# Attention row sums on Trainium2: a unit's last pair merged by DMA, two row sums a unit, the inverses moved

## The reference

```python
scores = jnp.einsum('bqhs,bkhs->bhqk', q, k) / np.sqrt(HEAD_DIM)
scores = jnp.where(context_mask[:, None, None, :], scores, -jnp.inf)
attn = jax.nn.softmax(scores, axis=-1)
out = jnp.einsum('bhqk,bkhs->bqhs', attn, v).reshape(B, Tx, C)
```

## Time and profile before

| what | us |
|---|---|
| median of 3 runs | 4442.11 (4439.8 to 4442.43) |
| the profiled execution | 4433.29 |
| its span, first to last instruction | 4431.5 |
| PE, DVE, ACT, POOL busy | 4264.6, 3400.1, 2850.1, 2938.9 |

### The profile page before, as it was taken

The page is one execution under the profiler, slowest core; times in us unless marked ns, Lnnn a source line. Parts: engine busy times, 40 slices in busy tenths (PEclk is TensorE's granted clock), DMA queues, the critical chain, the costliest instruction groups (busy, mean ns, idle before and its releaser), DMA issues.

```text
span 4431.5 us, 89201 instructions
## 1 busy us (share of the span) xinstructions
PE 4264.6 (96%) x36496; PEld 1486.4 (34%) x36496; DVE 3400.1 (77%) x3967; ACT 2850.1 (64%) x5184; POOL 2938.9 (66%) x1830
## 2 busy tenths in 40 slices
PE   4999999999999999999999999999999999999998
PEld 2322343223432234322342223422234222342223
DVE  5788667886688865888658886688866888668875
ACT  3387744877448864478655886558755587546884
POOL 2299652996539954499534995359953599426993
PEclk9999999999999999999999999999999999999999
DMA  5256642657326573356733566335664366543654
GB/s 182 71 121 125 158 143 62 125 119 187 115 62 128 115 200 102 71 117 124 191 101 77 115 125 184 106 79 119 124 174 110 78 122 127 167 112 78 126 124 107
DMA packets 193708, 539.67 MB, mean 122 GB/s; under 512 B 28737, under 2 KB 102785, under 8 KB 152082
## 3 DMA queue, kind: packets, MB, share of 16 engines
q0 software_dynamic: 43776, 318.79, 36.0%
q1 hardware_dynamic: 149522, 215.17, 15.6%
HBM read 118.32 MB, written 21.01 MB: 31 GB/s over the span
## 4 chain that ended last, share of the span: by engine, by line
PE 66%; DVE 20%; ACT 4%; DMA 3%; POOL 3%; issue 3%; SPq 0%; DVEq 0%; ACTq 0%; POOLq 0%
PE banks L1114 17%; PE banks L1126 16%; PE banks L1022 16%; PE banks L1082 11%; DVE max_parts L663 11%; PE banks L1157 4%; PE banks L991 2%; ACT region L892 2%; DMA sums<-wkT_wvT_wqT 1%; PE banks L1016 1%; POOL wkT_wvT_wqT L453 1%; DVE amax L611 1%; ACT values L972 1%; DVE x_stats L573 1%; DVE region L801 1%
## 5 line engine op out<-in xcount | busy, mean ns | idle before, releaser
L663 DVE TENSOR_REDUCE max_parts<-banks 128x2 f32<-128x1024 f32 x2048 | 2397.1, 1217 | 409.4 <-PE banks L1082 393.4
L892 ACT ACTIVATE region<-banks 128x512 f32<-128x512 f32 x4096 | 2190.5, 607 | 452.5 <-PE banks L1114 401.6
L453 POOL TENSOR_TENSOR wkT_wvT_wqT<-region 128x1024 f32<-128x1024 f32 x528 | 1313.0, 2632 | 464.6 <-PE banks L1126 273.0
L1114 PE MATMUL banks<-queries_stacked,keys_stacked 98*32 98x512 f16 x16384 | 1264.2, 382 | 12.5 <-ACT values L876 6.2
L1126 PE MATMUL banks<-region,values 128*32 128x512 f32 x8192 | 1076.0, 599 | 17.7 <-ACT region L892 14.2
L1082 PE MATMUL banks<-keys_stacked,queries_stacked 33*128 33x512 f16 x4096 | 724.0, 385 | 31.8 <-DVE max_parts L663 28.3
L1114 PEld LDWEIGHTS banks<-queries_stacked,keys_stacked 98*32 98x32 f16 x16384 | 401.3, 95 | 1000.3 <-ACT region L892 599.4
L1022 PE MATMUL banks<-region,wkT_wvT_wqT 128*128 128x512 f16 x2304 | 556.7, 380 | 13.2 <-DMA wkT_wvT_wqT<-weights_split 10.6
L1082 PEld LDWEIGHTS banks<-keys_stacked,queries_stacked 33*128 33x128 f16 x4096 | 184.2, 93 | 649.1 <-issue 354.1
L453 POOL TENSOR_TENSOR sums<-region 128x1024 f32<-128x1024 f32 x144 | 373.0, 2729 | 9.1 <-ACT region L892 9.1
L433 POOL TENSOR_TENSOR region<-row_sums_inverse,region 128x512 f16<-128x512 f32 x80 | 93.0, 1163 | 429.5 <-ACT region L855 428.9
(11 more groups left out here) (99 smaller groups left out, 3232.4 us busy)
## 6 DMA issues: line engine op xcount, KB each, us to landing
wdT<-wkT_wvT_wqT POOLq DMA_DIRECT2D x96, 1024.0 KB, 12.0
wkT_wvT_wqT<-wkT_wvT_wqT POOLq DMA_DIRECT2D x80, 1024.0 KB, 7.3
sums<-wkT_wvT_wqT POOLq DMA_DIRECT2D x72, 1024.0 KB, 7.4
wkT_wvT_wqT<-sums POOLq DMA_DIRECT2D x40, 1024.0 KB, 7.4
region<-in_x SPq DMA_DIRECT2D x24, 1024.0 KB, 8.6
wkT_wvT_wqT<-weights_split SPq DMA_DIRECT2D x8, 3072.0 KB, 20.6
keys_stacked<-region SPq DMA_DIRECT2D x384, 64.0 KB, 2.0
keys_stacked<-sums SPq DMA_DIRECT2D x384, 64.0 KB, 2.0
```

Of the source, the lines that this page charges most:

```text
L453: e.tensor_tensor(SUMS[dst][:, half], PR[i][:, half], PR[i + 1][:, half], ALU.add).then_inc(s_pr, 1)
L663: e.tensor_reduce(mpart[:, buf, :, a, t, c], MXB[parity], AX.X, ALU.max).then_inc(s_mxd, 1)
L892: e.activation(PR[u % 4][:, j * HALF:j * HALF + HALF], score_bank(m % NU, kt, j)[0], ACT.Exp, scale=SCALE).then_inc(s_ex, 1)
L1114: mm = e.matmul(dst[HD * t:HD * t + HD, :], KA[0:STR, ds(ka + (j * C + (u + 1) * P + HD * t), HD)], QA[0:STR, ds(qa[j], HALF)], start=True ...
```

## The change

- `buffers(n)` names six buffers. The last pair (tiles 14 and 15) goes into `sixth`, which is 5, 0 or 3 in turn, and `first`, `three` and `sixth` change places from unit to unit.
- A new `merge_pair` on GpSimd, at the start of units 1 to 6, merges the unit before's `sixth` into its `first` by an accumulating DMA. It stands right behind `merge_last`, and both now stand ahead of pair 0; `merge_last` stood between the halves of pair 0.
- PE makes two row sums in units 1 to 6: `SUMS[4]` in step 4, and `first` in step 5, when `merge_pair` has landed (`s_ap`).
- GpSimd normalises between the halves of pair 2, and pair 3 waits for `s_ap`.
- VectorE inverts the sums of the unit before last behind the maxima of step 4. In unit 6 the inverse of the unit before stays behind the next unit's maxima.
- The banks of the scores take turns a little differently: the stretch with two banks begins at tile 5 in place of 4.

```diff
-            if tile < 4:
+            if tile < 5:
                 return bank((7, 4, 5)[(4 * tile + j) % 3]), 3
...
-            return [(0, 1, 2, 3, 4), (3, 1, 0, 2, 4), (2, 1, 3, 0, 4)][n % 3]
+            if n == NU - 1:
+                return 3, 1, 0, 2, 4, None
+            first, three, last = [(0, 3, 5), (3, 5, 0), (5, 0, 3)][n % 3]
+            return first, 1, 2, three, 4, last
...
+                        def merge_pair():
+                            into, *_, src = buffers(2 * g + q - 1)
+                            e.wait_ge(s_acc, 3 * n * 16)
+                            e.wait_ge(s_pt, 2 * (b * (NU - 2) + 2 * g + q))
+                            e.dma_start(SUMS[into], SUMS[src], accum_op=ALU.add).then_inc(s_ap, 16)
...
-                        pair(0, first, merge_last if g + q > 0 else None)
+                        if g + q > 0:
+                            merge_last()
+                            merge_pair()
+                        pair(0, first)
                         pair(1, one)
                         merge(0, 1, one)
-                        if 2 <= 2 * g + q < NU - 1:
+                        def normalise():
                             e.wait_ge(s_inv, n - 1)
                             ao = AO[:, ds((2 * g + q - 2) * AO_UNIT, HALF)]
                             e.tensor_tensor(ao, ao, RL[:, :], ALU.mult).then_inc(s_an, 1)
-                        e.wait_ge(s_pv, n * KT + 4 + (3 if g + q == 0 else 4))
-                        pair(2, two)
+
                         if g + q > 0:
                             e.wait_ge(s_ac2, late * 16)
+                        pair(2, two, normalise if 2 * g + q >= 2 else None)
+                        if g + q > 0:
+                            e.wait_ge(s_ap, 16 * (b * (NU - 2) + 2 * g + q))
                         pair(3, three)
...
-                                e.tensor_tensor(SUMS[5][:, half], PR[2][:, half], PR[3][:, half],
+                                e.tensor_tensor(SUMS[sixth][:, half], PR[2][:, half], PR[3][:, half],
...
                             max_row(idx + 8 + 2 * t, 1 - q, QT + t)
+
+                            if n >= 2 and t == 0:
+                                invert_first(m - 2)
+                                invert_rest()
...
-                            if n > 0 and t == 2:
-                                invert_first(m - 1)
-                            if n > 0 and t == 3:
-                                invert_rest()
...
-                                if t == 3 and not end:
-                                    fresh = (s_ex, ex + 4 * J + 2)
-                                if t == 4 and not end:
-                                    sums = [(SUMS[5], (s_pt, 2 * (b * (NU - 2) + n)))]
-                                if t == closing:
+                                if t == (8 if end else 4):
                                     sums = [(SUMS[4], (s_ac2, 16 * (b * (2 * NU - 2) + 2 * n)))]
+                                if not end and t == 4:
+                                    fresh = (s_ex, ex + J + 2)
+                                if not end and t == 5:
+                                    sums = [(SUMS[buffers(n - 1)[0]], (s_ap, 16 * (b * (NU - 2) + n)))]
```

More of the change, by code:

```diff
@@ L182, in score_bank @@
                 slot = 4 * (KT * (n - NU + 2) + tile - 9) + j
-                return bank((4, 5, 0, 1, 2, 3)[slot % 6]), 2 if slot < 2 else 6 if slot >= 6 else None
+                return bank((5, 4, 0, 1, 2, 3)[slot % 6]), 2 if slot < 2 else 6 if slot >= 6 else None
             if n == 0 and tile < 8:
@@ L186, in score_bank @@
                 return bank((7, 4, 5)[slot % 3]), 3 if slot > 3 else None
-            if tile < 4:
+            if tile < 5:
                 return bank((7, 4, 5)[(4 * tile + j) % 3]), 3
             if tile < 8 or n == NU - 2:
-                return bank(4 + j % 2), 3 if tile == 4 and j < 2 else 2
+                return bank(5 - j % 2), 3 if (tile, j) == (5, 0) else 2
             slot = 4 * (tile - 8) + j + ((tile, j) >= (10, 2))
-            return bank((7, 4, 5)[slot % 3]), 2 if tile == 10 and j >= 2 else 3
+            return bank((7, 4, 5)[slot % 3]), 2 if tile == 10 and j >= 2 or (tile, j) == (8, 1) else 3
         def buffers(n):
-            return [(0, 1, 2, 3, 4), (3, 1, 0, 2, 4), (2, 1, 3, 0, 4)][n % 3]
+            if n == NU - 1:
+                return 3, 1, 0, 2, 4, None
+            first, three, last = [(0, 3, 5), (3, 5, 0), (5, 0, 3)][n % 3]
+            return first, 1, 2, three, 4, last
         s_w = sem("weights_loaded")
@@ L239, in build @@
         s_pt = sem("last_tiles_paired")
+        s_ap = sem("last_pairs_merged")
         s_wo = sem("out_projection_weights_loaded")
@@ L351, in _ @@
                         if 2 * g + q == NU - 1:
-                            e.wait_ge(s_pv, (b * NU + NU - 2) * KT + 4 + 5)
+                            e.wait_ge(s_pv, (b * NU + NU - 2) * KT + 4 + 6)
                             e.dma_start(WO[:, :, :], woT.rearrange("(c p) n -> p c n", p=P)).then_inc(s_wo, 16)
@@ L456, in pair @@
                                     halfway()
-                        first, one, two, three, second = buffers(2 * g + q)
+                        first, one, two, three, second, sixth = buffers(2 * g + q)
                         end = g == G - 1 and q == 1
@@ L516, in _ @@
                         if 2 * g + q < NU - 2:
-                            if g + q > 0:
-                                e.wait_ge(s_pv, n * KT + 4 + 5)
-                            elif b > 0:
+                            if g + q == 0 and b > 0:
                                 e.wait_ge(s_op, b * TT)
@@ L698, in last_sums @@
                     def last_sums(m):
-                        first, one, two, three, second = buffers(n)
+                        first, one, two, three, second, sixth = buffers(n)
                         late = b * (2 * NU - 2) + 2 * n
@@ L1201, in quad @@
                                     sums = [(PR[3], None)]
-                                if t == (2 if end else 3):
+                                if end and t == 2:
                                     sums = [(SUMS[buffers(n - 1)[0]], (s_acc, 48 * m))]
-                                if t == 3 and not end:
-                                    fresh = (s_ex, ex + 4 * J + 2)
-                                if t == 4 and not end:
-                                    sums = [(SUMS[5], (s_pt, 2 * (b * (NU - 2) + n)))]
-                                if t == closing:
+                                if t == (8 if end else 4):
                                     sums = [(SUMS[4], (s_ac2, 16 * (b * (2 * NU - 2) + 2 * n)))]
+                                if not end and t == 4:
+                                    fresh = (s_ex, ex + J + 2)
+                                if not end and t == 5:
+                                    sums = [(SUMS[buffers(n - 1)[0]], (s_ap, 16 * (b * (NU - 2) + n)))]
                             step(m, n, ex, ka, qa, v, u, t + 1, rows[u], sums=sums, fresh=fresh, closing=t == closing,
@@ L1217, in unit @@
                     ex, ka, v, rows = at(K3, J - 1, g + 1, q, not last)
-                    first, one, two, three, second = (SUMS[i] for i in buffers(n))
+                    first, one, two, three, second = (SUMS[i] for i in buffers(n)[:5])
                     for u in range(3):
```

## The result

The changed kernel takes **4606.65 us** (median of 4 runs, 4603.19 to 4611.13), against 4440.95 for the kernel before, measured beside it (4 runs, 4438.63 to 4442.43): ratio 1.0374, 95% interval 1.0356 to 1.0392. It is slower by 166 us. The forecast was 4512 in a range that ended at 4555: the sign was right, and the size was 95 us too small.

A forecast was written before the change was run, and what follows sets the result against it. The prediction took a closed loop of POOL and the DMA queue as the bound, 45.7 us per unit: 8.7 us more per batch entry, 70 over eight, on 4433.3 gives 4503, plus 8.8 gives 4512 us; range 4485 to 4555.

The forecast's parts named there:

- PE's bound, 42.6 us: One unit on PE alone: 44.26 us less 0.89 for a row sum and 0.77 for the moved inverse.
- the first two steps at 2.5: PE's first two steps of a unit: about 2.5 us each unless POOL holds them, from 2.91 and 2.86.
- The late merge's landing, 12.9: POOL's unit head: the late merge lands 12.9 us after its issue, second in the queue behind another merge.
- what POOL does until then: POOL has nothing to do from 9.9 us after the late merge's issue until its landing, about 3 us per unit.
- X to the start of pair 1: First part of POOL's loop, X being the issue of a unit's late merge: 18.8 us.
- Does PE add to the loop? ... I add nothing.: PE, stalled in step 5 for the new merge, keeps about 1 us in hand against POOL's pair 5: nothing added.
- tenths: PE's waits for ScalarE in steps 3 and 4: some tenths of a us.
- The inverse in step 4 at nothing: VectorE's inverse behind step 4's maxima: cost on PE taken as nothing, covered by the two row sums.
- What POOL's block costs: The wait for the late merge ahead of pair 0, no longer covered by pair 0's first half; whole change 70 us.
- PE's wait decides: Rival: merges landing 3 us later hold PE in step 5, units 2 us longer, about 4608 us; chance 0.10.
- The skill's rule: GpSimd transfers take about 2 us plus bytes at 436 GB/s: 1 MiB merge 4.4, second some 6 us.

The follow-up runs named there:

- e3_inverse: The kernel before with only the inverse and the normalisation moved as in the change: 4425.8 us, ratio 0.9972 to before.
- e5b_inverse_back: The changed kernel with the inverse back behind the maxima of steps 14 and 15, the normalisation left between the halves of pair 2: 4588.1 us.
- e4_block: The kernel before with its one merge_last moved ahead of pair 0, nothing else: 4518.6 us, ratio 1.0183 to before.
- e1_cover: The changed kernel with both merges put back between the halves of pair 0: 4491.8 us, ratio 1.0121 to before.
- e12_late_sum: e1_cover with PE's row sum of the first buffer moved from step 5 to step 7, with banks, copy and waits to match: 4452.2 us.
- e7b_fill_scores: The changed kernel with two real scores ahead of PE's stalls made seven times over in units 1 to 6: 4563.0 us.
- e2_fill: The changed kernel with twelve zero-weight matmuls per unit 1 to 6, ahead of PE's waits in steps 3 and 4: 4622.1 us.

## Why the prediction was wrong, step by step

- **PE's bound, 42.6 us, and the first two steps at 2.5.** The steps came out at 2.46 and 2.58, and the full-clock unit above has PE busy for 42.77. Right.
- **The late merge's landing, 12.9, and what POOL does until then.** Right: median 12.9, mean 12.69 from the issue, and about 3 us of idle time put to it. The step from the landing to pair 0 was mis-sized: POOL issued L481 0.62 us behind the landing (0.3 in the earlier trace rows), and X to the start of pair 1 was 19.2 in place of 18.8: about 21 us of the 103.
- **"Does PE add to the loop? ... I add nothing."** This is the step that failed. I followed PE only from the sixth merge's landing, into step 5, and asked whether it was in time for pair 5. The path that decided starts earlier: pair 0 frees the exponentials' buffer, ScalarE makes tile 4, PE does step 3, and on to tile 11. The chain of the changed kernel's profile goes that way:

```profile
2120.90 0.86 PE banks L1139 x8
...
2129.81 12.87 DMA wdT<-wkT_wvT_wqT
...
2145.31 4.71 POOL woT L457 x2
2150.07 0.47 issue
2150.53 0.60 ACT region L905
2151.18 0.52 PE banks L1127 x4
2151.70 1.71 PE banks L1139 x8
...
2171.51 0.24 PE banks L1127 x4
2171.77 0.61 ACT region L905
2172.38 2.46 POOL wkT_wvT_wqT L457
```

  It goes through PE and ScalarE from 2150.53 to 2172.38 and back to POOL's pair 5, and a step's value matmuls take 1.71 us at its start, where they took 0.86 a little earlier. At full clock "nothing" would have been right: in the 4 loops with no low clock this part takes 22.0 us (21.7 in the sum), and POOL's rows have no idle time in it but for its own pair. But PE stands some 2.5 us in step 3 of each unit (131.3 us of waits for ScalarE in the whole kernel), the granted clock drops to 1.2 GHz in 42 of 48 loops, and the part is then 1.0 to 2.8 us longer. I had called the waits in steps 3 and 4 "tenths" and asked nothing of what standing does to the clock. It makes up 80 of the 103 us that the loops are over their forecast; the clock's part of the miss is 44 to 66 us.
- **The inverse in step 4 at nothing.** Right for PE and wrong for POOL, whose normalisation waits for it where the clock is low, about 0.5 us a loop, a term that the chain had at nothing: e3_inverse shows the gain by itself, e5b_inverse_back a loss of 18.5 us beside the blocked pair 0.
- **What POOL's block costs.** Right in the main: e4_block, the block alone, costs 82 us, where the forecast had 70 for the whole change.
- **The rival "PE's wait decides"** had the time (4608) by luck, and half the place: PE did decide, but in step 3 for ScalarE, and not in step 5 for a merge 3 us late. The sixth merge landed at X + 26.1 where I had 26.4. Its price shows only with the block away: 74 us of waits in e1_cover, of which e12_late_sum takes 40 us out of the time.
- **The skill's rule** that I had weighed against the change's slowness (Trainium skill, DMA: Bandwidth & Descriptors, Anatomy of one DMA) was not borne out: the merges of 1 MiB landed after 6.9 us at the least, where the estimate by it was 4.4, and right behind another merge after 11.4 to 13.5, where it was some 6.

Three things stay open. The price of the clock lies between 44 and about 66 us. What else makes the loops longer than forecast at full clock, 0.5 us each in the changed kernel's own and 1.1 in e7b_fill_scores (46.83, of the loops that normalise), is located and not explained: POOL's start behind the landing, 0.3 us more of waiting for its own pair 1 (2574.95 to 2580.54 is 5.59 us in a loop with no low clock, where the sum had 5.27), and the two issues ahead of the next X, of which the first is followed by the second after 0.92 us in that loop, where the sum had 0.59. And in e12_late_sum PE's wait in step 3 was found and not tried.

## What to carry to other kernels

A wait put ahead of work is priced by following every engine that the work behind it releases, from that work on and not from the added instruction, and by asking what TensorE does meanwhile: where it stands for some us in each turn, the next rows may have to be reckoned at half the clock as well. Here 42 of 48 loops fell to it with PE standing for ScalarE 131 us in all, and 9 of 48 in e4_block with the same block, a row sum still in step 3 and 37.5 us of such waits. And a change of several parts is worth taking apart before it is judged: here one part, the inverse's move, was a gain of 0.3% by itself and a loss beside the rest.

## What the runs showed of the hardware that was not expected

- The clock can fall while PE's rows have no gap. In e2_fill PE was busy in all of 814.50 to 834.90, partly with zero matmuls of 32 rows, and ran at 0.50 of the clock for the second half; 98-row scores in the same place kept the low level to 27 us in the whole kernel. Whether the rows or the zeros made the difference was not tried.
- Making PE do more made the kernel faster: 4607 to 4563 us.
- A merge issued 0.6 us or so behind another landed after 10.9 to 14.4 us (medians of 12.3 to 13.0 in ten of the kernels here), and the one ahead of it after 6.9 to 9.8 (medians 7.0 to 7.6). One with no other issued within 1.3 us of it took from 6.9 to 13.3: the median is 7.4 to 7.9 in most kernels, and 8.5 to 8.6 in e1_cover and e12_late_sum.
